# First operand tiles loaded and converted in halves, two parameter broadcasts issued later, in a fused attention and feed-forward kernel

## The reference, cut to what matters

```python
query = q @ w_q.T          # q: layer-normalised x, (2, 512, 1024)
key   = k @ w_k.T          # k: the context, (2, 1024, 1024); w_k: (256, 1024)
value = v @ w_v.T          # v: the context
...
q2 = fake_quant(x2, x2_scale, x2_zp)   # layer 1 quantises the same context;
                                       # x2_scale, x2_zp are single numbers
```

## Time and profile before

| what | value |
|---|---|
| median of 3 runs | 1081.86 us (1080.81 to 1082.34) |
| the profiled execution | 1082.79 us |
| its span in the trace | 1081.0 us |
| busy share of PE, DVE, ACT, POOL | 96%, 81%, 61%, 9% |
| mean granted TensorE clock | 0.983 of full |
| PE's longest wait | 20.5 us, in `stage_e`, for ACT |
| the chain that ended last | DVE 8%, PE 2% of the span, all of it in `stage_e` |

### The profile page before, as it was taken

One profiled execution on the slowest core, in us unless ns is written; L12 is line 12 of the kernel. 1 busy time (PEld: TensorE's weight loads), 2 busy tenths in 40 slices (PEclk: granted clock), 3 DMA queues, 4 the chain that ended last, 5 costly groups with the idle time before them and its releaser, 6 DMA issues. The chain is left out here.

```text
span 1081.0 us, 20198 instructions
## 1 busy us (share of the span) xinstructions
PE 1036.2 (96%) x7174; PEld 782.8 (72%) x7174; DVE 873.5 (81%) x1880; ACT 663.4 (61%) x1126; POOL 93.0 (9%) x85
## 2 busy tenths in 40 slices
PE   8999999999999999999999999998999999956978
PEld 7878888777777777777777777765888887534647
DVE  5763544799999999999999999955774795879998
ACT  4332320498999889899989989942222114635837
POOL 0221011200000000000000000000003112400000
PEclk9999999999999999999999999999999999987989
DMA  8458779831133323212332321166315000000003
GB/s 330 176 162 293 258 262 277 316 116 43 39 74 73 73 68 73 52 35 63 73 73 68 73 59 33 38 240 233 118 59 170 0 0 1 1 1 1 1 1 155
DMA packets 55568, 112.95 MB, mean 104 GB/s; under 512 B 7724, under 2 KB 21164, under 8 KB 55388
## 3 DMA queue, kind: packets, MB, share of 16 engines
q1 hardware_dynamic: 55402, 112.10, 33.7%
q10 hardware_dynamic: 50, 0.16, 0.0%
q0 software_dynamic: 64, 0.00, 0.0%
HBM read 83.99 MB, written 27.26 MB: 103 GB/s over the span
## 5 line engine op out<-in xcount | busy, mean ns | idle before, releaser
L886 DVE CUSTOM_DVE_ANT_0 XS<-b_psS,b_mbias 128x1024 f32<-128x1024 f32 x256 | 310.9, 1215 | 0.9 <-PE b_psS L766 0.7
L841 ACT ACTIVATE XS<-XS,b_mins 128x1024 f32<-128x1024 f32 x256 | 295.8, 1155 | 10.1 <-DVE b_mins L886 9.5
L799 PEld LDWEIGHTS b_psT<-ident,XS 128*128 128x128 f32 x2048 | 230.0, 140 | 65.7 <-issue 47.6
L799 PE MATMUL b_psT<-ident,XS 128*128 128x128 f32 x2048 | 271.9, 276 | 1.7 <-ACT b_PT L849 1.7
L895 DVE COPY b_PT<-b_psT 128x512 f32<-128x512 f32 x256 | 176.8, 691 | 26.8 <-PE b_psT L799 24.9
L849 ACT COPY b_PT<-b_psT 128x512 f32<-128x512 f32 x256 | 149.5, 584 | 38.8 <-PE b_psT L799 30.8
L766 PE MATMUL b_psS<-XTh 128*128 128x512 f32 x512 | 155.9, 422 | 0.7 <-PEq L115 0.6
L780 PE MATMUL b_psO<-b_PT,XTh 128*32 128x256 f32 x1984 | 132.8, 385 | 0.0
L766 PEld LDWEIGHTS b_psS<-XTh 128*128 128x128 f32 x512 | 85.1, 189 | 18.5 <-DVE b_mins L886 7.7
L780 PEld LDWEIGHTS b_psO<-b_PT,XTh 128*32 128x32 f32 x1984 | 51.8, 109 | 42.1 <-issue 20.8
L416 ACT ACTIVATE a_oh<-a_psM 128x512 fp32r<-128x512 f32 x24 | 14.2, 595 | 81.4 <-PE a_psM L335 50.4
(11 more groups left out here) (268 smaller groups left out, 1616.6 us busy)
## 6 DMA issues: line engine op xcount, KB each, us to landing
XS<-in_ctx SPq DMA_DIRECT2D x16, 512.0 KB, 5.8
XTh<-QHd SPq DMA_DIRECT2D x32, 256.0 KB, 4.4
XTh<-QLd SPq DMA_DIRECT2D x32, 256.0 KB, 5.1
XS<-in_ctx_turned SPq DMA_DIRECT2D x8, 512.0 KB, 10.9
XS<-in_x SPq DMA_DIRECT2D x8, 512.0 KB, 11.4
a_wst<-in_L_xattn_w_q SPq DMA_DIRECT2D x8, 512.0 KB, 5.9
a_xn<-in_ctx_turned SPq DMA_DIRECT2D x8, 512.0 KB, 4.2
QHd<-a_oh SPq DMA_DIRECT2D x16, 256.0 KB, 5.5
```

Source lines behind the costliest of these rows:

```text
L799: last_t = pe.transpose(psT[:, kt, :], Pr[:, k % PR, kt * P:(kt + 1) * P], ident[:])
L841: act.activation(Pr[:, k % PR, :], Sc[:, k % 4, :], ACT.Exp, bias=mins[:, k % 4:k % 4 + 1], scale=-1.0, accum_out=sums[:, u, j:j + 1]).the ...
L886: dve.tensor_tensor_reduce(out=Sc[:, k % 4, :], in0=psS[:, k % 2, :], in1=mbias[:, qt, :], scale=1.0, scalar=3.4e38, op0=ALU.add, op1=ALU.min,
```

## The change

1. Weight tiles 0 and 1 and context tile 0 are loaded in two column halves (256 KB each) and converted half by half. A half of a weight tile is 4 of its 8 feature blocks; a half of context tile 0 is 512 of its 1024 context rows. SP, ACT and DVE all take: weights 0 first half, context 0 first half, context 0 second half, weights 1 first half, context 1 whole, weights 0 second half, weights 1 second half, context 2 and on.
2. `first_keys` takes `k` = 0 apart: for each weight tile and each half of the context rows three matmuls, with a wait of its own. The second halves of the weight tiles are waited for at `k` = 4.
3. POOL issues the two broadcast loads just before it waits for the scales of token tile 3, that is behind the third normalised tile.
4. The counts in the waits are raised to fit. In the later stages five semaphores are folded into others: `b_mbias_rest` and `b_one_ready` become `b_gp_ready`, `d_identb_ready` and `d_par_step` become `d_quant_setup`, and the count of `e_sink_near` is kept in `e_sink`. Each wait there still waits for the same instruction.

```diff
-            load_ctx0(0)
-            load_w(0)
-            load_w(1)
-            for k in range(1, KT):
+            load_first_w(0, PART[0])
+            for c, done in zip(PART, (c0_first, c0_in[0])):
+                sp.dma_start(XS[:, 0, c], ctxT[0:P, c]).then_inc(done, 16)
+            load_first_w(1, PART[0])
+            load_ctx0(1)
+            for w in range(2):
+                load_first_w(w, PART[1])
+            for k in range(2, KT):
                 load_ctx0(k)
...
-                for k in range(LATE):
-                    pe.wait_ge(c_split, k + 1)
+                for w in range(KVT):
+                    pe.wait_ge(w_split, w + 1)
+                    for n in range(2):
+                        pe.wait_ge(c_split, n + 1)
+                        for a, b in ((WTh, CTh), (WTh, CTl), (WTl, CTh)):
+                            pe.matmul(psM[:, 2 * w + n, :], a[:, w, 0, :], b[:, 0, PART[n]],
+                                      start=(a is WTh and b is CTh), stop=False)
+                for k in range(1, LATE):
+                    pe.wait_ge(c_split, k + 2)
                     for w in range(KVT):
-                        pe.wait_ge(w_split, w + 1)
+                        if k == KT // 2:
+                            pe.wait_ge(w_split, tile_parts(w))
...
-            ctx_hi(0)
-            weights_hi(0)
-            weights_hi(1)
-            for k in range(1, KT):
+            first_weights_hi(0, 0)
+            first_ctx_hi(0)
+            first_ctx_hi(1)
+            first_weights_hi(1, 0)
+            ctx_hi(1)
+            for w in range(2):
+                first_weights_hi(w, 1)
+            for k in range(2, KT):
                 ctx_hi(k)
...
-            pool.dma_start(qs[:, 0:1], quant[2].partition_broadcast(P)).then_inc(par, 16)
-            pool.dma_start(qs[:, 1:2], quant[3].partition_broadcast(P)).then_inc(par, 16)
             for t in range(NT):
+                if t == 3:
+                    pool.dma_start(qs[:, 0:1], quant[2].partition_broadcast(P)).then_inc(par, 16)
+                    pool.dma_start(qs[:, 1:2], quant[3].partition_broadcast(P)).then_inc(par, 16)
                 pool.wait_ge(scales_ready, t + 1)
```

More of the change, by code:

```diff
@@ L151, in stage_a @@
         w_in = [sem(f"a_w{u}") for u in range(2)]
+        w_first, c0_first = [sem(f"a_wf{u}") for u in range(2)], sem("a_c0f")
         q_in = [sem(f"a_q{u}") for u in range(2)]
@@ L195, in value_tile, with tile_parts @@
             return w - V0 if w < Q0 else KVT + w - V1
+        PART = (slice(0, HALF), slice(HALF, D))
+        KPART = (slice(0, KT // 2), slice(KT // 2, KT))
+        def tile_parts(w):
+            return w + 3
         def tile_view(staging, u):
@@ L203, in load_w, with load_first_w @@
                 src, r = weights(w)
-                if w >= 2:
-                    sp.wait_ge(w_split, w - 1)
+                sp.wait_ge(w_split, tile_parts(w - 2))
                 sp.dma_start(wst[:, w % 2, :], src[r * P:(r + 1) * P, :]).then_inc(w_in[w % 2], 16)
+            def load_first_w(w, cols):
+                src, r = weights(w)
+                done = w_first[w] if cols is PART[0] else w_in[w]
+                sp.dma_start(wst[:, w, cols], src[r * P:(r + 1) * P, cols]).then_inc(done, 16)
             def load_ctx0(k):
@@ L343, in first_keys @@
                 pe.wait_ge(mm_free, 4)
-                for k in range(LATE):
-                    pe.wait_ge(c_split, k + 1)
+                for w in range(KVT):
[7 more added lines that the diff above has]
+                    pe.wait_ge(c_split, k + 2)
                     for w in range(KVT):
-                        pe.wait_ge(w_split, w + 1)
+                        if k == KT // 2:
+                            pe.wait_ge(w_split, tile_parts(w))
                         for a, b in ((WTh, CTh), (WTh, CTl), (WTl, CTh)):
                             for n in range(2):
-                                pe.matmul(psM[:, 2 * w + n, :], a[:, w, k, :], b[:, k, n * HALF:(n + 1) * HALF],
-                                          start=(k == 0 and a is WTh and b is CTh), stop=False)
+                                pe.matmul(psM[:, 2 * w + n, :], a[:, w, k, :], b[:, k, PART[n]],
+                                          start=False, stop=False)
                 for w in range(KVT):
                     for k in range(LATE, KT):
-                        pe.wait_ge(c_split, k + 1)
+                        pe.wait_ge(c_split, k + 2)
                         for a, b in ((WTh, CTh), (WTh, CTl), (WTl, CTh)):
@@ L525, in quantise @@
                                   ).then_inc(q_step, 1)
[L527 to L530, removed]
+            first_weights_lo(0, 0)
+            first_ctx_lo(0)
+            first_ctx_lo(1)
+            first_weights_lo(1, 0)
+            ctx_lo(1)
+            for w in range(2):
+                first_weights_lo(w, 1)
+            for k in range(2, KT):
                 ctx_lo(k)
```

70 lines of the change are left out of this document (39 added, 31 removed).

## The result

| what | before | changed |
|---|---|---|
| median, same chip | 1082.01 us (20 runs) | 1079.65 us (20 runs) |
| ratio, 95% interval | | 0.9978 [0.9969, 0.9987] |
| profiled execution | 1082.79 us | 1079.49 us |
| its span | 1081.0 us | 1077.7 us |

The gain is 2.4 us. The forecast was 1077.3, a gain of 4.56, and the range ended at 1079.2: the kernel is faster, by half as much as forecast, and the time lies 0.45 us above the range.

The account below looks back on a forecast made before the run. PE was taken to bound the kernel, losing time in the opening: 0 at the start, −2.90 idle, −1.66 clock, 0 behind, −4.56 us in all, so 1081.86 − 4.56 = 1077.3 us. The range was 1076.0 to 1079.2.

Parts of the forecast that it names:

- What bounds the kernel, and why the second weight tile was late: Whole kernel and opening: PE bounds, busy 1036.2 of 1081.0 us; POOL's two broadcasts cost 2.9 us of transfer.
- Rival 1: Opening: broadcasts do not cause the DMA lull, which stays; gain 3.0 us (1078.8), or 1.4 (1080.5) if the clock falls; chance 0.08.
- rival 5: Opening: identity matmuls set PE's start, so if loads were already in time nothing moves, 1081.9; chance 0.03.
- Rival 3: Opening: half of weight tile 1 or context 1 late enough that the clock still falls, 1.66 less, 1079.0; chance 0.04.
- The opening's loss, 2.90 idle and 1.66 at half pace: PE's first 60 key matmuls: 2.90 us idle and 1.66 us at 1.2 GHz, together 4.56 us, all to be gained.
- A half costs 0.63 us: Opening loads: a half tile transfers in 0.63 us, half of the full 1.28; at full price the gain is 3.5 us.
- The cover of 1.5 us: Opening: context 1 ready at 9.5 us, PE needing it at 11.0, so PE never waits.
- All that follows, the turns of token tiles and the stores, is released by PE, ACT and DVE in a fixed order, so it shifts along. I cost it at nothing.: Behind the opening: everything later moves earlier with PE, nothing of the 4.56 us is lost; cost 0.
- Rival 2: Halves not half price, or gain given back to a load or token tile that did not move; up to 1079.3; chance 0.08.
- Broadcasts at their new place, cost nothing: POOL before token tile 3: issues take at most 2 × 0.75 us; landing has 6.3 us of cover before DVE asks; cost 0.
- Rival 4: Broadcasts land late at their new place, DVE's reciprocal waits; gain gone at 21.8 us landing, 1084 at 24; chance 0.03.
- The chances: Forecast 0.74, rivals 1 to 5 0.08, 0.08, 0.04, 0.03, 0.03; below 1079.7 (forecast, rivals 2, 3, half of 1) 0.88.

Follow-up runs that it names:

- keys first: Changed kernel, SP storing the last three key products of the first stage ahead of the quantised tile and the values: 1079.58 us, ratio 0.9955.
- the second set of runs: The changed kernel run again, unaltered, against the kernel before on another chip: 1079.53 us, ratio 0.9976.
- the load moved: SP's load of the eleventh context tile to be quantised issued ahead of the scores loads; on the changed kernel 1078.4 and 1078.29 us, on the kernel before 1082.61.
- keys first too: Changed kernel with key stores ahead of quantised tile and values, and the eleventh context tile's load ahead of the scores loads: 1078.38 us, ratio 0.9950.
- load alone: Changed kernel with only the eleventh context tile's load issued ahead of the scores loads, stores in their old order: 1078.4 us, run again 1078.29.
- the kernel before with keys first: Kernel before, with only the last key stores of the first stage moved ahead of the quantised tile and the values: 1082.0 us, ratio 0.9992.
- the two with keys first: Kernel before with key stores ahead of quantised tile and values: 1082.0 us; the same plus the eleventh context tile's load ahead of scores loads: 1082.64 us.

## Why the prediction was wrong, point by point

- **What bounds the kernel, and why the second weight tile was late.** Right, and shown: the broadcasts make the lull (broadcasts alone: 406 GB/s at 6 us; halves alone: 117). Rival 1 falls, and so does rival 5. Rival 3 (the clock still falls, 1079.0) lies near the median and falls too: the granted clock is 1.00 in the stretches above.
- **The opening's loss, 2.90 idle and 1.66 at half pace.** Right: the opening gained 4.37 us, 0.19 less than forecast, with a start 0.28 earlier than before and 14.14 us from there to the second loop, forecast 13.7. Second loop 22.18 for 22.0, first value product 30.34 for 30.1.
- **A half costs 0.63 us.** Wrong, and of little consequence by luck. This term was mis-sized: ACT takes the parts at these times.

```profile
3.69 0.63 ACT L423 ACTIVATE WTh<-a_wst 128x512 fp32r<-128x512 f32 x1 [1.68 <-DMA a_wst<-in_L_xattn_w_k]
5.00 0.63 ACT L427 ACTIVATE CTh<-XS 128x512 fp32r<-128x512 f32 x1 [0.68 <-DMA XS<-in_ctx_turned]
6.40 0.63 ACT L427 ACTIVATE CTh<-XS 128x512 fp32r<-128x512 f32 x1 [0.78 <-DMA XS<-in_ctx_turned]
7.34 0.63 ACT L423 ACTIVATE WTh<-a_wst 128x512 fp32r<-128x512 f32 x1 [0.30 <-DMA a_wst<-in_L_xattn_w_k]
8.74 1.06 ACT L419 ACTIVATE CTh<-XS 128x1024 fp32r<-128x1024 f32 x1 [0.77 <-DMA XS<-in_ctx_turned]
```

  The halves stand 1.31, 1.40 and 0.94 us apart, whole tiles 1.28 us. Context 1 comes at 8.74 instead of 7.2, its low part is done at 11.06, and PE takes it at 11.11, where I had it ready at 9.5. The cover of 1.5 us was gone: PE's starts step by 0.47 us there instead of 0.23, and in three of the five other executions with halves and late broadcasts the view of waits has PE waiting for context 1, 0.2 (twice) and 0.4 us. The conversions themselves cost 0.63 (ACT, forecast 0.60) and 0.69 us (DVE, as forecast).
- **"All that follows, the turns of token tiles and the stores, is released by PE, ACT and DVE in a fixed order, so it shifts along. I cost it at nothing."** This is the step that failed: the forecast had nothing lost behind the opening, and 1.2 us were. It is true for 137 us. At the end of the stage the order is held by SP and by landings: the `in_ctx` load sits behind 18 other issues, and the store of the keys behind that of the values. The loss was 1.2 us in the profiled execution, 0.5 in two others and 1.0 with keys first. The profile before showed it: a copy with 4.91 us of waiting for a DMA where its neighbour waits 4.84 for PE, and POOL standing 23.05 us for a load. I read only the rows of the opening for what is late next. Rival 2 named this case ("part of the gain is given back to a load or a token tile that did not move") and let it reach 1079.3; it got 0.08, because I had not read the end of the stage.
- **Broadcasts at their new place, cost nothing.** Right. Timelines of POOL and DVE, changed kernel:

```profile
38.14 0.75 POOL L648 DMA_DIRECT2D a_qs<-in_L_xattn_x_scale  x1
38.89 0.57 POOL L649 DMA_DIRECT2D a_qs<-in_L_xattn_x_zp  x1
39.50 1.21 POOL L653 TENSOR_SCALAR a_xn<-XS,a_rstd,a_nmr 128x1024 f32<-128x1024 f32 x1
...
53.51 0.15 DVE L609 RECIPROCAL a_qinv<-a_qs 128x1 f32<-128x1 f32 x1
```

  The token tile behind them is 0.5 us late against PE, and the reciprocal has no wait in front of it, 14.6 us after the second issue began. The DMA view of the changed kernel, 36 to 56 us (tiles, queue, count, KB, us to landing), and the stretch from 38 to 44 us:

```profile
a_qs<-in_L_xattn_x_scale POOLq DMA_DIRECT2D x1, 0.5 KB, 3.4
a_qs<-in_L_xattn_x_zp POOLq DMA_DIRECT2D x1, 0.5 KB, 3.7
```

```profile
38.00:44.00 6.00, 6.00 (x33) 5.08 (x32) 5.41 (x12) 2.12 (x3) 2.67 (x4) 1.00 0.42 123
```

  DVE is busy for 5.41 of these 6 us, and the broadcasts land in 3.4 and 3.7 us, faster than the 8.1 beside the opening's loads. The delay that the Trainium skill warns of ("SBUF — State Buffer", "Who interferes with whom") is not seen at this place; whether DVE used its two-port mode there no row says. Rival 4 falls.
- **The sum against the measurement.** The median is 2.35 us above the forecast. 0.19 is the opening, 1.23 the handover, and 0.16 came back behind it: 1.26 of the missing gain is in the traces. The other 1.09 is not in them: the profiled execution of before stood 0.93 us above the median that I subtracted from, that of the changed kernel 0.16 below its own. So 3.30 us between the profiles are 2.4 between the medians. In the second set of runs the change gave 2.87 us. The range had room for about 1.9 us above the forecast, enough for either of the two and not for both at once. The chances have a slip as well: forecast, rivals 2 and 3 and half of rival 1 are 0.90, not 0.88.

**The clock farther on.** In two of the profiled executions with the load moved (keys first too: 3.75 to 5.56 us; load alone: 4.47 to 6.33) PE's lead over before grew by 1.8 and 1.9 us between 752 and 976 us, in two others by 0.4 and 0.1. The stretches say where most of it comes from. PE waits once near 752 us in `stage_cd`, and the clock falls behind that wait in some executions. A row of PE's timeline and a stretch, before and then changed with the load moved:

```profile
756.07 0.77 PE L1321 MATMUL c_psT<-c_TS,c_Et 120*128 120x512 f32 x2 [2.46 <-DVE c_Et L1664]
758.00:760.00 2.00, 2.00 (x6) 1.58 (x5) 1.85 (x4) 1.06 (x1) 0.00 (x0) 0.50 0.00 0
```

```profile
751.60 0.73 PE L1368 MATMUL c_psT<-c_TS,c_Et 120*128 120x512 f32 x2 [2.15 <-DVE c_Et L1711]
752.00:754.00 2.00, 2.00 (x10) 1.63 (x9) 1.63 (x3) 1.30 (x2) 0.00 (x0) 1.00 0.12 33
```

From this matmul to the next `c_psT` pair are 7.63 us before (756.07 to 763.70) and 6.03 here (751.60 to 757.63), so 1.6 of the 1.8 and 1.9 us are the clock. It fell there in the changed kernel too, both times. The fall does not go with the change: it is missing in the kernel before with keys first as well. So the profiled executions of 1077.36 and 1076.57 us flatter their kernels by it.

The clock also makes the openings of kernels with whole tiles and the broadcasts at the head differ by up to 1.6 us from one execution to the next. In the two with keys first the granted clock is still 0.50 in 16 to 18 us, where before has 1.00 in 16 to 17. The rest is PE's wait for weight tile 1, 2.6 to 3.3 us. Of four such executions, that of the kernel before has the shortest opening.

**What stays open.** Why one issue of a weight load takes 1.69 us in one execution and 0.45 in the next. In the first, a packet of 16 KB of an instruction queue was on a DMA engine for 1.4 us at 154.26, just among the last query stores; in the kernel before one stands at 156.56, between stores. In the traces of five of the thirteen profiled executions such a packet is on an engine while SP makes the issue behind the last query store or the one after it. In those five that issue takes 1.20 to 2.17 us and ends 0.16 to 0.37 us behind the packet. In the other eight the packet is over before, and the weight load's issue takes 0.44 or 0.45 us. That the packet holds up SP's issue fits these times and was not tried. Also open is why PE's wait in the opening and the length of the slow stretch differ from one execution to the next.

## What to carry to other kernels

When an early stage gets shorter, look for the next place where a queue of transfers, and not an engine, sets a time: in the profile before it was a wait that ended 0.07 us behind PE, with a DMA named as its end, and an engine off the path that had stood 23 us for one load. Such a tie cost nothing before and ate 0.5 to 1.2 us of the gain after; an issue order that looks harmless (a load behind 18 others) is the thing to change together with the opening. And the price of a tiny load on the software queue is what the big transfers beside it lose: here two loads of 0.5 KB cost the opening over 4 us. Before trusting a difference of 1 to 2 us between two profiled executions, compare the granted clock of their stretches.

## What the runs showed of the hardware

- Two broadcasts of one number to 128 partitions, issued by GpSimd at 1.7 us, hold the large transfers down for some 3 us: 33 GB/s at 7.0 to 7.5 us before, 117 and 139 in 6 to 8 us with halves alone. Without them the same stretch carries 406 and 418 GB/s of whole tiles. The packets of the software queue took 0.9% of the DMA engines' time in it, so it is not their own time that is lost.
- The first loads of a stream in halves of 256 KB run at 320 to 387 GB/s in 6 to 8 us in six executions, where whole tiles run at 393 to 418 in two; in 5 to 6 us it is 193 to 313 against 397 and 422. Halving a load did not halve its time.
- After a halt of PE of 2.5 us the granted clock stood at 1.2 GHz when it resumed (halves alone, 13 to 14 us), as after 2.63 us before. Near 752 us it fell with halts of 2.18 us (keys first) and 2.46 us (before), and stayed at 2.4 GHz with halts of 2.15, 2.20 and 2.55 us (load alone, keys first with load, kernel before with keys first), so the length of the halt alone does not tell.
- The packets of an instruction queue, 16 KB, were on a DMA engine for 0.9 to 1.8 us between 152 and 159 us. In the five executions where one was on it during the issue behind the last query store or the one after it, that issue took 1.20 to 2.17 us instead of 0.45.
